# The bias fill of a tile moved from its start to its middle, between the third maximum block and the third score block

## The reference, cut to what matters

```python
qkv = (gn(x).reshape(B, S, dim) @ qkv_w + qkv_b)      # q, k, v per head
attn = einsum('bqc,bkc->bqk', q * scale, k)
rel_h = einsum('bhwc,hkc->bhwk', r_q, Rh)             # 48 values per query
rel_w = einsum('bhwc,wkc->bhwk', r_q, Rw)             # 48 values per query
attn = softmax(attn + rel_h[..., :, None] + rel_w[..., None, :])
x = x + (attn @ v) @ proj_w + proj_b
```

## Time and profile before

| what | value |
|---|---|
| median of 3 runs | 7006.76 us |
| the profiled execution | 7003.42 us, its span 7001.6 us |
| busy share of the span | PE 98%, DVE 78%, ACT 66%, POOL 13% |
| granted clock of PE, mean | 0.989 of full speed |
| bias fills | 1152, each read by one copy on ACT |

### The profile page before, as it was taken

One profiled execution on the slowest core, in us unless ns is written; L12 is line 12 of the kernel. 1 busy time (PEld: TensorE's weight loads), 2 busy tenths in 40 slices (PEclk: granted clock), 3 DMA queues, 4 the chain that ended last, 5 costly groups with the idle time before them and its releaser, 6 DMA issues.

```text
span 7001.6 us, 139199 instructions
## 1 busy us (share of the span) xinstructions
PE 6841.4 (98%) x53600; PEld 4298.1 (61%) x53600; DVE 5486.4 (78%) x10165; ACT 4650.1 (66%) x10033; POOL 934.5 (13%) x967
## 2 busy tenths in 40 slices
PE   7999999999999999999999999999999999999998
PEld 4666666666666666666665666656666566666664
DVE  6887888778887788877888778887787878877883
ACT  2667676666666676666766666667676666766765
POOL 2112010110102110111111111102101121101110
PEclk8999999999999999999999999999999999999999
DMA  5666676666667666666666666766667666666663
GB/s 142 142 148 155 134 150 144 155 154 133 152 133 158 149 138 154 142 162 138 145 143 147 153 142 141 153 146 154 143 139 152 139 159 142 139 148 144 144 145 93
DMA packets 306306, 1013.72 MB, mean 145 GB/s; under 512 B 107440, under 2 KB 196976, under 8 KB 215920
## 3 DMA queue, kind: packets, MB, share of 16 engines
q1 hardware_dynamic: 305648, 1004.81, 64.4%
HBM read 745.26 MB, written 255.69 MB: 143 GB/s over the span
## 4 chain that ended last, share of the span: by engine, by line
PE 93%; DMA 3%; DVE 2%; issue 0%; SPq 0%; ACT 0%; POOL 0%; POOLq 0%; DVEq 0%; ACTq 0%
PE work L791 31%; PE work L782 27%; PE work L861 26%; PE work L807 4%; DMA moving<-rel_scratch 3%; PE work L826 2%; PE work L845 2%; DVE mpart L660 1%; PE work L834 1%; PE work L813 0%; DMA qk_scratch<-back 0%; DVE xb L651 0%; ACT probs L547 0%; DVE stats L610 0%; POOL back L495 0%
## 5 line engine op out<-in xcount | busy, mean ns | idle before, releaser
L660 DVE TENSOR_REDUCE mpart<-work 128x1 f32<-128x512 f32 (+1 forms) x8640 | 5091.4, 631 | 1217.2 <-PE work L791 1196.8
L547 ACT ACTIVATE probs<-work 128x512 f32<-128x512 f32 (+1 forms) x8640 | 4047.8, 557 | 951.4 <-PE work L782 936.8
L782 PE MATMUL work<-moving,keys 113*128 113x512 f32 (+1 forms) x8640 | 3395.8, 394 | 78.8 <-DMA moving<-rel_scratch 73.7
L791 PE MATMUL work<-mkeys,hi 128*128 128x512 f32 (+1 forms) x8640 | 3451.7, 401 | 11.8 <-DVE mpart L660 8.6
L791 PEld LDWEIGHTS work<-mkeys,hi 128*128 128x128 f32 x8640 | 1647.8, 191 | 1152.4 <-DVE mpart L660 866.8
L861 PE MATMUL work<-probs,vall 128*17 128x288 f32 x27648 | 2016.3, 409 | 0.0
L782 PEld LDWEIGHTS work<-moving,keys 113*128 113x128 f32 x8640 | 1645.7, 191 | 534.4 <-ACT probs L547 141.4
L861 PEld LDWEIGHTS work<-probs,vall 128*17 128x17 f32 x27648 | 637.4, 97 | 803.2 <-ACT probs L547 245.0
L480 POOL TENSOR_TENSOR full<-full,hi 128x384 f32<-128x384 f32 x576 | 580.8, 1009 | 1417.0 <-DVE hi L705 1417.0
L530 ACT ACTIVATE full<-work 48x384 f32<-48x384 f32 x576 | 279.3, 486 | 604.5 <-PE work L807 604.5
L535 ACT ACTIVATE full<-work 48x384 f32<-48x384 f32 x576 | 278.9, 484 | 583.6 <-PE work L807 583.6
(11 more groups left out here) (42 smaller groups left out, 649.1 us busy)
## 6 DMA issues: line engine op xcount, KB each, us to landing
moving<-rel_scratch SPq DMA_DIRECT2D x1728, 144.0 KB
moving<-qk_scratch SPq DMA_DIRECT2D x288, 576.0 KB
rel_scratch<-hi SPq DMA_DIRECT2D x192, 432.0 KB, 5.9
rel_scratch<-full SPq DMA_DIRECT2D x192, 432.0 KB, 5.5
moving<-rel_scratch SPq DMA_DIRECT2D x288, 288.0 KB
image<-qk_scratch SPq DMA_DIRECT2D x384, 144.0 KB, 4.2
keys<-qk_scratch SPq DMA_DIRECT2D x192, 288.0 KB, 4.8
qk_scratch<-split_hi SPq DMA_DIRECT2D x144, 192.0 KB, 3.8
```

The lines of the kernel that those rows point to most:

```text
L547: act.activation(probs[:, tile % RING, lo:up], bank[:, 0:up - lo], ACT.Exp).then_inc(act_read, 1)
L660: dve.tensor_reduce(mpart[:, u % 2, q, m:m + 1], bank[:, 0:MSPLIT[m][1] - MSPLIT[m][0]], AX.X, ALU.max)\
L782: pe.matmul(bank[:, 0:up - lo], tile_of(keys[0:K_ROWS, u % 2, :], c, third), moving[0:K_ROWS, slot_of(u, third)[0], lo:up], start=True, st ...
L791: pe.matmul(bank[:, 0:up - lo], hi[:, u % 2, q * P:(q + 1) * P], mkeys[:, u % 2, lo:up], start=True, stop=True).then_inc(for_dve, 1)
```

## The change

The bias fill of tile t is appended to the items of place 2 and no longer to those of place 0. Nothing else is edited. Since all engines and all waits take their numbers from the same table, the fill, its copy on ACT and the bank numbers move together.

```diff
             if t < 12 and u + 2 < UNITS:
-                plan[u][t][0].append(("rel", u + 2, t))
+                plan[u][t][2].append(("rel", u + 2, t))
```

## The result

| | before | after |
|---|---|---|
| median | 7004.44 us (20 runs, 6994.69 to 7012.8) | 7017.64 us (20 runs, 7010.83 to 7062.7) |
| ratio | | 1.0018, 95% interval 1.001 to 1.0026 |
| the profiled execution, its span | 7003.42, 7001.6 us | 7019.38, 7017.6 us |

The change makes the kernel 13 us slower, with an interval of 7 to 18 us. The forecast was 6 us slower, in a range from 7001 to 7030 us.

A forecast was written before the change was run, and what follows sets the result against it. The prediction took PE's train of matmuls, busy 98% of the span, as the bound. Early tiles +9 us and late tiles -3 us made +6 us: 7009 us for the profiled execution, 7013 us as median (+0.09%), range 7001 to 7030.

The forecast's parts named there:

- The bound and the frame: Only longer or shorter PE matmul trains count, through the fill's cost behind M2 and waits for banks whose pairs change.
- The fill costs the same in either place: On PE, the fill costs the same behind M2 as behind M0: 0, within -0.01 to +0.01 us a tile.
- S2's wait: In early tiles (0 to 5), S2's load just meets the end of S0's exponential: 0.00 to 0.01 us.
- S3's wait: In early tiles (0 to 5), S3's load waits for S1's exponential: 0.02 us a tile over 435 tiles, +9 us.
- S4 and the late tiles: S4 loses nothing in early tiles; in late tiles (6 to 11) waits for ACT are met, giving back -3 us.
- Tile 1 and the maximum banks: Tile 1 stays at 3.87 us, since M1's maximum starts behind DVE's copies; its stall swallows S3's 0.02.
- DVE's room pays: Rival: M1's earlier start shortens tile 1's stall, 0.21 us x 94 = 20 us, time 6984 us; chance 0.04.
- Units j = 3: In these units, where DVE also has statistics, PE's grace is used up similarly; no loss and no gain counted.
- Ahead of the loop: In the two units ahead of the loop there are no scores and DVE sets the pace; no cost counted.
- The rival with dearer waits: Score banks close up: S2 and S3 wait 0.05 us longer, 0.07 a tile, +30 us, 7037 us; chance 0.15.

The follow-up runs named there:

- e3: The changed kernel with the exponentials of S0 and S1 in tiles 0 to 5 reading 448 of their 512 columns; 7008.1 us, ratio 1.0004.
- e1: The kernel before with only the fills of tiles 0 to 5 moved to place 2; 7016.4 us, ratio 1.0017.
- e9: The kernel before with only the fills of the two units ahead of the loop moved to place 2; 7008.3 us, ratio 1.0006.
- e10: The changed kernel with the fills of the two units ahead of the loop back at place 0; 7012.7 us, ratio 1.0009.
- e12: The kernel before with the exponentials of S0 and S1 in tiles 0 to 5 reading 448 of 512 columns; 7006.0 us, ratio 1.0003.
- e8: The kernel before with all fills moved to place 3, between M3 and S3; 7025.6 us, ratio 1.0027.
- e7: The kernel before with all fills moved to place 1, between M1 and S1; 7018.8 us, ratio 1.002.
- e2: The kernel before with only the fills of tiles 6 to 11 moved to place 2; 7004.4 us, ratio 0.9999.
- e4: The kernel before with x's loads moved to tiles 0, 1 of units j=1 and its stores to tiles 0, 1 of j=3; 6931.9 us, ratio 0.9895.
- e5: The changed kernel with the transfers of x moved as in e4; 6939.5 us, ratio 0.9907.
- e6: e4 with the fills of tiles 6 to 11 at place 2 and those of tiles 0 to 5 at place 0; 6934.3 us, ratio 0.9897.
- e11: e4 with the fills of tiles 6 to 11 of the loop at place 3, all other fills at place 0; 6927.9 us, ratio 0.9892.

## Why the prediction was right, and where its size was off

- **The bound and the frame.** Right in the main: PE's train sets the time, and the loss in the loop comes through the pairs of the score banks. It isn't the only way: DVE's earlier start and the part ahead of the loop count too, as below.
- **The fill costs the same in either place.** Right: R to the next maximum block is 0.48 before, 0.49 after, and e3 has early tiles of before's length with the fill in the middle.
- **S2's wait, 0.00 to 0.01.** Right at its low end: the load starts at PE's own pace, also where S0's read is over sooner.
- **S3's wait, 0.02 an early tile, +9 us.** Right: 1.79 from M0, M4 at 2.13, 0.0205 us a tile. e1 has it alone, e3 takes it away with -9.5 us.
- **S4 and the late tiles, -3 us.** Right in sign, and smaller: 0.023 a unit, -2 us. The ACT waits of these tiles are gone but for 12 of 734.
- **Tile 1 and the maximum banks.** Right: 3.87 us before and after, with the same last wait. "DVE's room pays" is refuted for tile 1, where it was placed.
- **Units j = 3, "no loss there and no gain".** Wrong: a term put at nothing. DVE's room does pay there, in tiles 7, 9 and 12, 0.8 us a unit, -6 us. It is as large as the whole forecast. The prediction looked at the statistics in tiles 0 to 5 of these units and not at the rest of the norm behind them.
- **Ahead of the loop, 0.** Wrong, by a small sum: "In the two units ahead of the loop there are no scores, and DVE sets the pace" holds only while PE is at full clock. It is on the slow one for part of that stretch, where a fill between M2 and M3 leaves DVE without work, and the clock rose at 117 us instead of 108. It is +2 us (e9, e10).
- **The rival with dearer waits, +30 us.** The reads ended where the plain tile had them, so its condition was never met. The hand-over of 0.05 us also held at the new places (2530.23 to 2530.29, 2521.71 to 2521.76): from the end of the exponential to the load it is 0.050 to 0.052 us in all 766 such waits before and in all 543 after.

With the terms as measured, +9 - 2 - 6 + 2, the sum is +3 us, where the forecast had +9 - 3. That the forecast of +6 is near it is in part luck, since the term that it left out in units j = 3 is partly made up by the one that it left out ahead of the loop. The measured 13 us lie outside this sum: their interval begins at 7. What holds up is the mechanism of the early tiles (e1, e3, e12, e8) and with it most of the loss; the balance doesn't close.

How far it stays open can be told. e1 meets the sum of its parts (+11 for +11), and so do e9 and e12 and, with all fills at place 1, e7, within 2 us. The kernels with late fills at place 2 all lie above theirs: the changed kernel +13 for +3, e2 -1 for -4, e3 +3 for -3, e10 +7 for +4, and against e4, e5 +7.5 for +2.5 and e6 +2.4 for -6. With them at place 3, e8 has +21 for +10, and e11 -4 for -10 against e4. For e2, e3 and e10 the sum is inside the interval of the time, for the changed kernel and e8 it is outside, and all the gaps have one sign. So a gain in the tiles of j = 3 may not reach the time, or the late fills may cost something that single tiles don't show, perhaps in the stalls for `rel_scratch`. No run here tells which.

## What to carry to other kernels

Moving work within a ring of buffers moves the pairs of who waits for whom, so list these pairs for the new order and put each on the clock of a tile that already has that order. Then go through the stretches with another bound, here units j = 3 and the part ahead of the loop, since the start of another engine's work moves too. An insertion that takes a slot of the ring should stand where the slots it brings together are far apart in time: here near the attend, the one long stretch without a score block. The 13 us under study were a sixth of what moving the transfers of x to other tiles gave.

## What the runs showed that I had not expected

- A wait of 0.19 us on a weight load costs 0.02 us: S3's load started 0.14 us after M3, where it usually starts with it, and M4 was 0.02 late. So about 0.12 us of delay is hidden behind the running matmul here. The two waits of 0.16 and 0.18 us in the late tiles cost 0.004 a tile.
- The change of an order within a tile delayed the rise of PE's clock from 1.2 to 2.4 GHz ahead of the loop: granted clock 0.96 and 1.00 with the fill at place 0, 0.54 and 0.68 with it at place 2, in the same 11 us.
- Two loads and two stores of 864 KB a stage, issued in tiles 9 and 10, cost 73 us more than in tiles 0 and 1, through stalls in tile 14, four to five tiles later, and the slow clock behind them (15 such tiles in the profile before, 6.7 to 12.7 us long instead of 3.9). In their new place the loads still bring a stall of tile 7.
- The same shift by one position costs PE time where ACT is waited for and gives it back where DVE is: M1's maximum starts 0.43 us earlier, which is worth nothing in most tiles and 0.2 to 0.3 us in three tiles of the units where DVE sets the pace.
